# Two LoRA layers on one core: three result slots instead of two, x turned on VectorE, selections moved between engines, program unrolled

## What is computed

```
x1 = x  + x @ W^T + bias + (x @ A0[i]^T) @ B0[i]^T      i: one of 32 adapters, one per batch, rank 16
y  = x1 + (x1 @ B1[j]^T) @ A1[j]^T                      j: one of 8 adapters, one per batch, rank 16
```

## Time and profile before

| | us |
|---|---|
| median of 3 runs | 113.35 (112.4 to 113.79) |
| the profiled execution, device time | 111.63 |
| its span | 109.9 |
| busy: PE / PE weight load / VectorE | 99.7 / 97.6 / 70.3 |
| busy: ScalarE / GpSimd | 48.1 / 49.2 |

### The profile page before, as it was taken

One profiled execution on the slowest core, in us unless ns is written; L12 is line 12 of the kernel. 1 busy time (PEld: TensorE's weight loads), 2 busy tenths in 40 slices (PEclk: granted clock), 3 DMA queues, 4 the chain that ended last, 5 costly groups with the idle time before them and its releaser, 6 DMA issues.

```text
span 109.9 us, 2662 instructions
## 1 busy us (share of the span) xinstructions
PE 99.7 (91%) x726; PEld 97.6 (89%) x726; DVE 70.3 (64%) x244; ACT 48.1 (44%) x128; POOL 49.2 (45%) x81
## 2 busy tenths in 40 slices
PE   5980999969989797999999999999999999999990
PEld 5880999969979796999999999999999999999980
DVE  0055395957369679677767676776767577776351
ACT  4037555746261534453625444352735445362210
POOL 6303397005466737344535464544536455440400
PEclk9999589999999999999999999999999999999999
DMA  3999999883804274652747375464838465460223
GB/s 48 387 311 209 338 365 267 206 218 43 270 23 121 97 225 144 197 198 85 222 117 261 80 253 157 154 191 122 246 102 256 124 202 168 143 216 0 101 84 107
DMA packets 11766, 19.39 MB, mean 176 GB/s; under 512 B 1360, under 2 KB 5840, under 8 KB 11600
## 3 DMA queue, kind: packets, MB, share of 16 engines
q1 hardware_dynamic: 10480, 14.04, 42.2%
q0 software_dynamic: 1280, 5.28, 17.4%
HBM read 13.47 MB, written 5.84 MB: 176 GB/s over the span
## 4 chain that ended last, share of the span: by engine, by line
PE 60%; DMA 19%; issue 6%; DVE 4%; SPq 4%; POOL 2%; ACT 1%; DVEq 1%; POOLq 0%; ACTq 0%
PE psum L437 42%; PE psum L476 9%; DMA w_rows<-in_L_cond_base_weight 7%; DMA gathered_rows<-by_rank,rows_now_odd 7%; PE psum L400 4%; DMA by_rank<-row_ends 4%; SPq L207 3%; PE psum L467 3%; PE psum L382 2%; DVE a_by_rank L644 1%; POOL gathered_rows L276 1%; DVE g_sel L674 1%; POOL w_rows L295 1%; DVE y L697 1%; ACT wd L546 1%
## 5 line engine op out<-in xcount | busy, mean ns | idle before, releaser
L437 PE MATMUL psum<-wd,xt 128*128 128x256 f32 (+1 forms) x384 | 65.6, 314 | 1.1 <-DVE y L697 1.1
L437 PEld LDWEIGHTS psum<-wd,xt 128*128 128x128 f32 x384 | 56.3, 189 | 1.7 <-DVE y L697 1.1
L282 POOL TENSOR_TENSOR up_rows<-gathered_rows,up_rows 128x512 fp32r<-128x512 f32 x16 | 20.6, 1288 | 21.6 <-ACT up_rows L546 21.2
L546 ACT ACTIVATE up_rows<-gathered_rows 128x512 fp32r<-128x512 f32 x16 | 10.2, 635 | 31.5 <-PE psum L437 24.6
L546 ACT ACTIVATE wd<-table_rounded 128x128 fp32r x64 | 14.6, 300 | 4.1 <-issue 4.0
L623 DVE TENSOR_TENSOR xt<-psum,xt 128x512 fp32r<-128x512 f32 x16 | 11.0, 690 | 7.4 <-ACT xt L546 7.4
L697 DVE TENSOR_TENSOR y<-psum,bias_all 128x512 f32<-128x512 f32 x15 | 10.4, 692 | 8.5 <-PE psum L476 6.9
L476 PE MATMUL psum<-up_rows,u_sel 128*128 128x256 f32 x96 | 13.9, 280 | 0.0
L476 PEld LDWEIGHTS psum<-up_rows,u_sel 128*128 128x128 f32 x96 | 12.9, 188 | 0.0
L674 DVE COPY g_sel<-gathered_rows 16x16 f32 x64 | 12.1, 190 | 0.6
L276 POOL DMA_INDIRECT gathered_rows<-by_rank,rows_now_even x8 | 8.1, 1017 | 6.5 <-POOL rows_now_even L273 6.5
(11 more groups left out here) (64 smaller groups left out, 81.7 us busy)
## 6 DMA issues: line engine op xcount, KB each, us to landing
x_in<-in_x SPq DMA_DIRECT2D x16, 256.0 KB
out<-y SPq DMA_DIRECT2D x15, 256.0 KB, 2.8
bw_rows<-in_L_cond_lora_B_w SPq DMA_DIRECT2D x1, 1024.0 KB, 4.9
w_rows<-in_L_cond_base_weight SPq DMA_DIRECT2D x2, 512.0 KB, 8.8
a_rows<-in_L_cond_lora_A_w SPq DMA_DIRECT2D x1, 1024.0 KB, 11.3
by_rank<-bw_by_rank SPq DMA_DIRECT2D x4, 256.0 KB
by_rank<-row_ends SPq DMA_DIRECT2D x1, 330.0 KB
b_rows<-in_L_cond_B SPq DMA_DIRECT2D x1, 256.0 KB, 5.0
```

The source lines that it names most:

```text
L282: nc.gpsimd.tensor_tensor(out=up_rows[:, slot, LO, :], in0=gathered_rows[:, slot, 0:D], in1=up_rows[:, slot, HI, :], op=ALU.subtract).then ...
L437: last = nc.tensor.matmul(psum[:, 2 * slot + half, start:end], xt[:, slot, c, x_part, :], wd[:, w_part, c, col:col + end - start], start=( ...
L546: return nc.scalar.activation(dst, src, ACT.Copy)
```

## The change

The diff replaces most of the kernel's body. What it does:

1. The hardware loops are written out on all engines.
2. There are three result slots in PSUM (banks 2-3, 4-5, 0-1) and three y buffers instead of two, so block k waits for the result of block k-3. `u_blocks` moves from SBUF to PSUM.
3. x is loaded in groups of 1, 1, 2, 4, 4 and 4 blocks as squares, [32 rows, batch, 128 columns] for each quarter of the columns (runs of 512 bytes), and turned by one VectorE instruction for each block, 128x512 from SBUF to PSUM. PE's transposes of x go. Contraction row p of chunk c is now column 4p+c, and the tables are transposed with that stride.
4. G is selected on GpSimd by four multiplications of 128x16 with a mask, and both down tables are selected on ScalarE.
5. The gathered rows have four buffers, and three gathers are issued before the first block. The copy of the row numbers before each gather goes.
6. In the start-up W is loaded first (after B1), then B0. The order on PE becomes B1, W, C1, B0, G, first block, A0. The first blocks' orders are written by hand on each engine.

```diff
+X_GROUPS = ((0, 1), (1, 2), (2, 4), (4, 8), (8, 12), (12, 16))
+GATHERS = 4
-        U, EDGE_U, XT = 4, 5, 7
+        SLOT_BANK = (2, 4, 0)
+        U, XT = banks[6], banks[7]
+        u_blocks = U[:, P:2 * P]
 # SyncE, first loads
-            sp.dma_start(bw_rows[:, :, :], ...).then_inc(bw_in, 16)
             sp.dma_start(b1_rows[:, :], ...).then_inc(b1_in, 16)
+            for half in range(2):
+                oc = slice(half * C // 2, (half + 1) * C // 2)
+                sp.dma_start(w_rows[:, oc, :], w_view[:, oc, :]).then_inc(w_in[half], 16)
+            sp.dma_start(bw_rows[:, :, :], ...).then_inc(bw_in, 16)
...
 # GpSimd
+            def g_select(k):
+                pool.wait_ge(gathered[k % GATHERS], 16 * (k // GATHERS) + 16)
+                if k >= 2:
+                    pool.wait_ge(gh_filled, k - 1)
+                n1 = adapters_of(pool, k, L1)
+                for b in range(NB):
+                    last = nc.gpsimd.tensor_tensor(
+                        out=g_sel[:, k % 2, b, L1, :], in0=gathered_rows[:, k % GATHERS, bass.ds(n1[b] * R + G_COL, R)],
+                        in1=batch_mask[:, b, 0:R], op=ALU.mult)
+                last.then_inc(g_ready, 1)
...
+            gather(0)
+            gather(1)
+            gather(2)
+            for k in range(NBLK):
+                g_select(k)
+                up_low(k)
+                if k + 3 < NBLK:
+                    gather(k + 3)
 # PE, after the start-up
+            for k in range(3, NBLK - 1):
                 wait_x(k)
-                transpose_x(pair + slot, 1 - slot)
                 wait_d(k)
-                if y_free:
-                    pe.wait_ge(y_ready, k - 1)
+                wait_slot(k)
                 base(k, [0])
                 add_gh(k - 1)
                 base(k, range(1, C - 1))
                 up(k - 1)
                 base(k, [C - 1])
 # ScalarE
+            select(1, L0)
+            up_high(0)
+            select(2, L0)
+            xt_high(2)
+            u_high(0)
+            select(2, L1)
+            up_high(1)
+            for k in range(2, NBLK - 1):
+                select(k + 1, L0)
+                u_high(k - 1)
+                xt_high(k + 1)
+                select(k + 1, L1)
+                up_high(k)
 # VectorE
+            def x_turn(k):
...
+                nc.vector.transpose(out=XT.rearrange("p (c b s) -> p b c s", c=C, b=NB),
+                                    in_=x_squares[:, k * NB:(k + 1) * NB, :].rearrange("p b (i c) -> p b c i", c=C),
+                                    ).then_inc(xt_filled, 1)
...
+            x_turn(2)
+            turn_u(0)
+            xt_low(2)
+            own_u(0)
+            u_low(0)
+            for k in range(2, NBLK):
+                turn_u(k - 1)
+                own_u(k - 1)
+                if k + 1 < NBLK:
+                    x_turn(k + 1)
+                u_low(k - 1)
+                if k + 1 < NBLK:
+                    xt_low(k + 1)
+                if k == 2:
+                    finish(0)
+                if k < NBLK - 1:
+                    finish(k - 1)
```

More of the change, by code:

```diff
@@ L198, in _, with store_by_rank @@
                              ids_of.rearrange("(a k b) -> a k b", a=1, b=NB)).then_inc(ids_in, 16)
[L201 to L204, removed]
+            def store_by_rank(by_rank_part, n, row):
                 for c in range(C):
@@ L234, in _, with adapters_of @@
                 sp.wait_ge(y_ready, NBLK + half)
-                sp.dma_start(out_blocks[NBLK - 1, :, cols], y[:, 1, cols]).then_inc(y_stored[1], 16)
-            sp.wait_ge(y_stored[0], 16 * (NBLK // 2))
-            sp.wait_ge(y_stored[1], 16 * (NBLK // 2 + 1))
+                sp.dma_start(out_blocks[NBLK - 1, :, cols], y[:, (NBLK - 1) % SLOTS, cols],
+                             ).then_inc(y_stored[(NBLK - 1) % SLOTS], 16)
+            for s in range(SLOTS):
+                stores = len(range(s, NBLK, SLOTS)) + (s == (NBLK - 1) % SLOTS)
+                sp.wait_ge(y_stored[s], 16 * stores)
+        def adapters_of(engine, k, layer):
+            _, values = nc.values_load_multi_w_load_instructions(
+                ids[0:1, k, layer, :], engines=[engine.engine], min_val=0,
+                max_val=(N0, N1)[layer] - 1,
+                skip_runtime_bounds_check_because="the inputs index the adapter tables")
+            return values
         @block.gpsimd
@@ L265, in _ @@
             nc.gpsimd.memset(row_ends[:, :, BB_COL - D:ROW - D], 0.0).then_inc(zeros_ready, 1)
[L266 to L296, removed]
+            nc.gpsimd.tensor_copy(row_ends[:, GROUPS - 1, 0:P], ident[:, :]).then_inc(zeros_ready, 1)
             pool.wait_ge(bias_all_in, 16)
@@ L362, in _ @@
             pe.wait_ge(ident_ready, 1)
+            pe.wait_ge(b1_in, 16)
+            for c in range(C):
+                last = nc.tensor.transpose(fill_of("b1")[:, c * P:(c + 1) * P], b1_rows[:, c * P:(c + 1) * P],
+                                           ident[:, :])
+            last.then_inc(filled, 1)
+            for oc in range(C):
+                if oc % 2 == 0:
+                    pe.wait_ge(w_in[oc // 2], 16)
+                pe.wait_ge(w_plus, oc + 1)
+                for c in range(C):
+                    last = nc.tensor.transpose(fill_of(f"w{oc}")[:, c * P:(c + 1) * P],
+                                               chunk(w_rows[:, oc, :], c), ident[:, :])
+                last.then_inc(filled, 1)
@@ L363, in _ @@
+            wait_drained(pe, "b1")
+            for h in range(2):
+                for c in range(C // 2):
+                    for oc in range(C):
+                        last = nc.tensor.matmul(fill_of(f"c1_{h}")[:, c * P:(c + 1) * P],
+                                                chunk(w_rows[:, oc, :], h * C // 2 + c), b1_cols[:, oc, :],
+                                                start=(oc == 0), stop=(oc == C - 1))
+                last.then_inc(filled, 1)
             pe.wait_ge(bw_in, 16)
-            for q in range(4):
+            for q, before in enumerate(("b1", "w0", "w3", "c1_0")):
+                wait_drained(pe, before)
@@ L480, in up @@
                         last.then_inc(out_filled, 1)
-            def step(pair, slot, y_free=True):
-                k = pair * 2 + slot
+            wait_drained(pe, "bw3")
+            for g in range(4):
+                for oc in range(C):
+                    last = nc.tensor.matmul(fill_of("g")[:, g * P:(g + 1) * P], bw_cols[:, oc, g * P:(g + 1) * P],
+                                            b1_cols[:, oc, :], start=(oc == 0), stop=(oc == C - 1))
+            last.then_inc(filled, 1)
@@ new lines, in _ @@
+            wait_drained(pe, "w3")
+            wait_x(0)
+            base(0, range(C), with_d=False)
+            pe.wait_ge(a_in, 16)
+            for g, before in enumerate(("bw1", "bw2", "bw3", "c1_1")):
+                wait_drained(pe, before)
+                for c in range(C):
+                    last = nc.tensor.transpose(fill_of(f"a{g}")[:, c * P:(c + 1) * P],
+                                               chunk(a_rows[:, g, :], c), ident[:, :])
+                last.then_inc(filled, 1)
@@ new lines, in _ @@
+            wait_drained(pe, "a2")
+            wait_x(1)
+            base(1, range(C), halves=[1])
+            wait_drained(pe, "g")
+            wait_d(0)
+            for c in range(C):
+                for n, (x_part, d_part) in enumerate(HALVES):
+                    last = nc.tensor.matmul(EDGE_U, xt[:, 0, c, x_part, :], wd[:, d_part, c, D_AT[0]:D_AT[0] + P],
+                                            start=(c == 0 and n == 0), stop=(c == C - 1 and n == 2))
+            last.then_inc(u_filled, 1)
@@ L485, in step @@
+            wait_d(1)
+            base(1, range(C - 1), halves=[0])
+            add_gh(0)
+            base(1, [C - 1], halves=[0])
+            wait_x(2)
+            wait_d(2)
+            pe.wait_ge(u_blocks_ready, 1)
+            base(2, [0])
+            up(0)
+            add_gh(1)
+            base(2, range(1, C - 1))
+            up(1)
+            base(2, [C - 1])
+            for k in range(3, NBLK - 1):
                 wait_x(k)
-                transpose_x(pair + slot, 1 - slot)
@@ L546, in copy, with xt_high, select @@
                 return nc.scalar.activation(dst, src, ACT.Copy)
-            for q in (1, 3):
-                act.wait_ge(filled, BW_FILL + q + 1)
-                copy(ranks_of_bw(q), by_rank(BW_FILL + q, N0)).then_inc(act_drained, 1)
+            def xt_high(k):
+                act.wait_ge(xt_filled, k + 1)
+                if k >= 2:
+                    act.wait_ge(u_filled, k - 1)
+                copy(xt[:, k % 2, :, HI, :], chunked(XT)).then_inc(xt_hi_ready, 1)
+            def select(k, layer):
+                ready, table = ((sel0_ready, table0_rounded), (sel1_ready, table1_rounded))[layer]
+                if k >= 2:
+                    act.wait_ge(u_filled, k - 1)
+                n = adapters_of(act, k, layer)
```

(48 more changed lines are left out.)

481 lines of the change are left out of this document (205 added, 276 removed).

## The result

| | kernel before | changed kernel |
|---|---|---|
| median of 4 runs, us | 112.88 | 117.16 |
| ratio to before, 95% interval | | 1.033 (1.023 to 1.043) |
| profiled execution, device time / span | 111.63 / 109.9 | 115.32 / 113.5 |

The forecast was 110.8 us, with a range from 106.2 to 114.6. The kernels have a faster and a slower state and each ratio compares executions in the faster one, so it is not exactly the ratio of the medians. The steady part gained 3.3 us where 2.1 were forecast; the start-up lost 7.0 where 0.4 were to be won.

What follows compares the result with a forecast made beforehand. PE alone was taken to bound 12 of 16 blocks, with the wait for tables before them; steady part -2.1 and start-up -0.4 gave -2.5 us, device time 109.1, scaled to 110.8 against 113.35, range 106.2 to 114.6.

Steps and rivals of the forecast that it cites:

- The steady part: PE's steps from block 4 on: transposes removed -4.84 us, waits for u +2.76, together -2.1; step 4.69.
- the start-up: Everything before block 3, dated by its longest path: block 3 at 42.3 against 42.70, so -0.4 us.
- 0.23 given back for u: Before add_gh in each steady step: PE waits 0.23 us for u_own without the transposes as cover; 2.76 in all.
- a bound on GpSimd: Rival in the steady steps: g_select costs 2.0 instead of 1.26, GpSimd's round 5.4; +6.9 us, 117.7; chance 0.14.
- u_own at 0.92: Rival in the steady steps: own_u takes 0.92 instead of 0.35 beside GpSimd's remainder; +6.8 us, 117.6; chance 0.04.
- a slow x_turn: Rival in the steady steps: x_turn beyond 1.3 us, not 0.72, holds up xt and PE; 113.5; chance 0.04.
- The gather's 0.8 us before its start: GpSimd's steady round: 1.30 us from up_low's end to gather's start, less 0.2, kept within a 4.65 round.
- C1's 32 matmuls take 3.74: Start-up on PE after W: C1's products take 3.74 us, from 7.9 to 11.65, before B0 is transposed.
- From the table's completion to the first use, 5.19 less 0.2: First gather in the start-up: 5.19 us as today less the 0.2 row-number copy, first use at 30.8.
- Clock: I take 0.8: PE's pause before block 2: the fall to 1.2 GHz costs 0.8 us, between 0 and 1.7.
- my list: Start-up from the gathered rows' first use to block 2: selections, xt, own_u and add_gh sum to 5.5 us.
- late table: Rival in the start-up: SP's store pace stays slow, table at 29.1, block 3 3.2 later; +0.7, 114.1; chance 0.15.

Runs made afterwards that it cites:

- e5: Changed kernel with the first pass of base chunk 1 (two matmuls) ahead of add_gh in steps 3 to 14; 1.005 of the kernel before.
- e10: Changed kernel with x_turn reading its columns in order instead of every fourth; measured once, 116.51 us.
- e12: Changed kernel with the edits of e6 and e5 together, rerun in more rounds; 0.945 of the kernel before, 106.6 us.
- e1: Changed kernel with C1's products reading W in contiguous 128-column pieces instead of every fourth column; 1.0035 of the kernel before.
- e9: Kernel before with C1's products reading every fourth column of W as stationary operand; 1.0139 of the kernel before.
- e2: Changed kernel with x blocks 2 and 3 loaded before the table's stores, blocks 4 to 7 after the third gather landed; 0.992 of the kernel before.
- e11: Changed kernel with only x blocks 4 to 7 held back until the third gather has landed; 1.012 of the kernel before.
- e4: Changed kernel with 20 more float32 products of zeros on PE in the pause before the first add_gh; 1.017 of the kernel before.
- e3: Changed kernel with the edits of e1 and e2 together; 0.981 of the kernel before.
- e6: Changed kernel with e2's x loads and the start-up reordered so the table's copies and B0 precede C1's halves; 0.971 of the kernel before.

## Why the prediction was wrong

**The steady part was right.** Forecast: 0.44 us of transposes gone and 0.23 given back for u, a step of 4.69. Measured: a wait of 0.21 and a step of 4.63; e5 took the wait away and got 4.44, where the forecast has 4.46. Of the 1.2 us won beyond the forecast, 0.7 are these steps and 0.25 is block 3's first chunk, 1.13 us in the kernel before, where PE came to it from a wait, and 0.87 now; the rest lies in the last two blocks. The rivals about a bound on GpSimd, u_own at 0.92 and a slow x_turn all fell: u_own took 342 to 352 ns in all 16 blocks, and four masked selections took 0.75, not 0.87. x_turn, though, took 1.11 and not the 0.72 forecast; it fitted only because VectorE has room, and e10 shows that its 0.39 too much is the same oversight as C1's below. The gather's 0.8 us before its start, which I carried into GpSimd's round, was the wait for the row-number copy and went with it (0.15 now). u_own is the clearer for a second reading. In the kernel before, a GpSimd remainder running over it lengthened it, to 0.92 where they overlapped by 0.77 us and here, by 0.48, to 0.62:

```profile
42.01 1.28 POOL L282 TENSOR_TENSOR up_rows<-gathered_rows,up_rows 128x512 fp32r<-128x512 f32 x1 [0.32 <-issue]
...
42.81 0.62 DVE L685 SCALAR_TENSOR_TENSOR u_own<-u_blocks,bb_sel,batch_mask 128x128 f32<-128x128 f32 x1
```

In the changed kernel the overlap is below 0.1 us in 13 of 16 blocks and says little. In e12 it is 0.2 to 0.35 in 13 of 16 blocks, and u_own never takes more than 0.35:

```profile
47.21 1.30 POOL L338 TENSOR_TENSOR up_rows<-gathered_rows,up_rows 128x512 fp32r<-128x512 f32 x1 [2.10 <-ACT up_rows L527]
...
47.90 0.35 DVE L628 SCALAR_TENSOR_TENSOR u_own<-psum,gathered_rows,batch_mask 128x128 f32<-128x128 f32 x1
```

That u_own stays at 0.35 with one input in PSUM is what the Trainium skill says (SBUF — State Buffer, "Who interferes with whom"): these traces agree.

**The start-up was wrong in three terms of its sum**, which gave block 3 at 42.3 instead of 49.7:

- *C1's 32 matmuls take 3.74.* They took 7.47. I took the price of a contiguous operand from the row and did not ask what `chunk(...)`, every fourth column, does to a weight load. +3.7, shown by e1 and, in the other kernel, by e9. The Trainium skill has the rule that I overlooked: SBUF — State Buffer, in "Door 1: The DMA port swizzle", says that SBUF is read in lines of 16 bytes and that an access pattern which goes to a new line with every element pays, without a figure for it. Four float32 are one line, which is exactly this stride; 329 against 192 ns and 1.115 against 0.717 us agree with it.
- *From the table's completion to the first use, 5.19 less 0.2.* It took 37.34 - 29.39 = 7.95. I had noted that x comes up to four blocks early, "so I cost it at nothing". It is the early issue that costs: SyncE puts 1.5 MB in front of the first gather, for which add_gh(0) and all blocks behind it wait. +3.0, shown by e2 and e11.
- *Clock: I take 0.8.* The pause was 5.5 us and the loss, 1.8, stood fully on the path. +1.0, e4.

Two smaller terms nearly cancel: the stores, begun at 19.89, took 5.7 us back to back where the forecast leaves 5.0 from the first copy at 16.1 to 21.1, +0.7, and the table's last store landed in 3.76, 1.0 less than the 4.74 of the earlier trace rows. From first use to block 2, by my list 5.5, it was 5.35 (37.34 to 42.69). Together that is the 7.4 us between 42.3 and 49.7: the order of dependences was read rightly, and the prices put on some of its links were not.

The "late table" rival had the table complete at 29.1, and it was at 29.39, but this is luck: it gives SyncE's pace as the reason, 8.3 us for stores that took 5.7, and C1's 3.7 are not in it. I gave no case to a start-up late by more than 3.2 us, though the whole chain before block 2 hung on dates that I had worked out without a row for the new forms. The range was too narrow for that.

## What to carry to other kernels

When a layout is changed so that one engine's work falls away, price every other reader of the new layout in its own form: a row for the contiguous shape is no price for the strided one. Ask of each early bulk load which small, urgent transfer it now stands in front of. And where a chain of tables gates everything, put what leads to the last store first on every engine; here that order, the held-back load and two matmuls ahead of add_gh turned +3.3% into -5.5%.

## What the hardware showed that I had not expected

- Stationary float32 operands of 128x128 read with a stride of 16 bytes load in 329 ns instead of 192, and products bound by them take twice the time (7.47 against 3.74 us for 32), at full clock, in two kernels.
- A float32 32x32-block transpose of 128x512 on VectorE, from SBUF to PSUM, takes 0.72 us read in order and 1.11 with that stride.
- The first indirect gather of 128 rows landed in 3.6 to 4.0 us with no x load issued just ahead of it (e2, e3, e6, e12), in 3.9 behind 0.5 MB (e11) and in 6.9 behind 1.5 MB of loads on another queue; two further gathers issued behind it made no difference to it.
- u_own, 128x128 on VectorE, took up to 0.92 us beside a GpSimd instruction with both its large inputs in SBUF, and 0.35 with one of them in PSUM.
- Gathers issued one after the other with no copy between them start 0.30 us after the end of the one before, against 0.8 behind the copy of a row number.
